# Attention scores: two heads from each half of the partitions, products that alternate between the halves, and a PSUM copy placed behind the second maximum

## Chip, cores and metric

The kernel runs on one core of a Trainium2 chip. The time is the device time of one execution in microseconds (us); lower is better. TensorE is written PE in the profile, its weight loads PEld, VectorE DVE, ScalarE ACT, GpSimd POOL and SyncE, which issues the DMAs here, SP.

## What is computed

The input is 8 x 256 tokens of 256 features in float32. The whole is six residual blocks in a row: mixture of experts, a selective scan, the mixture again, a gated feed-forward, causal attention, and the feed-forward again. Only the attention is touched. Cut to that, the reference is:

```python
slopes = get_slopes(16)                                   # 16 heads of 16 features
q = split_heads(x @ Wq + bq); k = split_heads(x @ Wk + bk); v = split_heads(x @ Wv + bv)
attn = einsum('bhqd,bhkd->bhqk', q, k) / sqrt(16)
attn = attn + (-slopes[:, None, None] * (Tx - 1 - arange(Tx))[None, None, :])
attn = where(causal, attn, finfo(float32).min)
p = softmax(attn, axis=-1)
out = einsum('bhqk,bhkd->bhqd', p, v) ... @ Wo + bo
```

## The kernel before

The attention works on four chunks of 512 tokens, which are two sequences of 256. A unit is four heads of one sequence: `unit(n)` gives the chunk c, the block kb of 128 features (eight heads), the sequence b and the half, and there are 32 units in all, N = 32. The q and k rows of a head are stacked over partitions, as hi, hi and lo parts against hi, lo and hi parts, with two more rows for the position bias: 50 partitions, `ROWS`. `attn_stack` has one head of each pair in partitions 0 to 49 and the other in 64 to 113. A unit takes the four heads of one of these halves.

Queries and keys of a sequence are cut at 128. For each head there are three blocks of 128 x 128: the early queries against the early keys (bank 0 of PSUM), and the late queries against both (banks 1 and 2). What is above the diagonal gets -1e30 by a matmul of the identity (`one`) with the mask.

TensorE (`tensor`, line 1938) runs in iteration n: `scores(n + 2)`, a job of slot 0, `turn(n)`, `weigh(n - 1)`, a job of slot 1. `scores` (line 1975) makes four early products and their mask and signals `s_SA`; it waits for the second exponentials (`s_exp`) of the unit before, makes four late products and two masks, and signals `s_S`. `turn` (line 2000) transposes the twelve blocks of probabilities into banks 3, 4 and 5, and waits before each bank until it has been copied out; the third, t = 2, waits for `s_pt2.at(n)`, the copy of unit n - 1. `weigh` (line 2017) multiplies the transposed probabilities with v. A job, by the table `JOBS`, is one of: a projection of q or k for the next chunk (six matmuls of 512 columns), of v, the output projection, or four transposes of a layer norm ("ln").

VectorE (`vector`, line 2201) runs in iteration n, in this order: the reciprocal of unit n + 1, `first(n + 2)`, the row maxima over bank 0; `keep(n - 1)`, the copy of bank 5 into `attn_pT`, which signals `s_pt2`; `second(n + 2)`, the maxima over banks 1 and 2; then parts of the layer norm, the low halves of the outputs, and its share of the jobs (for q or k this is `rows_lo`, which waits for ScalarE's `rows_hi`).

ScalarE (`scalar`, line 2116) runs in iteration n: four exponentials over bank 0 (line 2156), four over banks 1 and 2 (line 2162), each after the respective maxima, then jobs and the copies of banks 3 and 4 (`keep`, line 2166). GpSimd divides the probabilities by their sums (line 1882), two calls a unit. SyncE brings the stacks of the next chunk in.

Each engine runs its instructions in the order in which they are written. Score banks 0, 1 and 2 exist once, banks 3 to 5 once too.

Of the kernel before, what the change touches and what calls it, by code (L numbers as in the profile page):

```python
# [22 lines left out]
P = 128  # L23
# [5 lines left out]
KB = HID // P  # L29
# [1683 lines left out]
class Attention:  # L1713
# [18 lines left out]
    def __init__(self, k, tag, ins, before, tail, rows, fixed):  # L1732
        self.k, self.ins, self.before, self.tail = k, ins, before, tail
        self.rows, self.fixed = rows, fixed
        k.kind = tag
        self.s_load, self.s_wh, self.s_wl = Sem(k, "load"), Sem(k, "wh"), Sem(k, "wl")
        self.s_fix, self.s_kept, self.s_fill = Sem(k, "fix"), Sem(k, "kept"), Sem(k, "fill")
        self.s_one, self.s_bo = Sem(k, "one"), Sem(k, "bo")
        self.s_in, self.s_hi, self.s_lo = Sem(k, "in"), Sem(k, "hi"), Sem(k, "lo")
        self.s_row = [Sem(k, f"row{i}") for i in range(2)]  # L1740
        self.s_stack = [[Sem(k, f"stack{i}_{kb}") for kb in range(KB)] for i in range(2)]
        self.s_SA, self.s_S, self.s_nA, self.s_nB = Sem(k, "SA"), Sem(k, "S"), Sem(k, "nA"), Sem(k, "nB")
        self.s_eA, self.s_exp, self.s_rec = Sem(k, "eA"), Sem(k, "exp"), Sem(k, "rec")
        self.s_p, self.s_T = Sem(k, "p"), Sem(k, "T")
        self.s_pt01, self.s_pt2, self.s_pv = Sem(k, "pt01"), Sem(k, "pt2"), Sem(k, "pv")
        self.s_vp, self.s_v = Sem(k, "vp"), Sem(k, "v")
        self.s_oH, self.s_oL, self.s_out = Sem(k, "oH"), Sem(k, "oL"), Sem(k, "out")
        self.prior, last = {}, ("v1", 0)
        for c in range(NCH):
            for u in range(self.UNITS):  # L1750
                for slot in range(2):
                    job = self.job(c, u, slot)
                    if job:
                        self.prior[job], last = last, job
        self.prior["out1", NCH - 1] = last

        a = Arena(k, tag)
        new = a.new
        self.pt = new("pT", [P, 2, 3, CHUNK])
        self.p0, self.p1 = new("p0", [P, 3, 4, P]), new("p1", [P, 3, 4, SEQ])  # L1760
        self.v = new("v", [P, 4, self.PAIRS, 3 * HD])
        assert a.off <= k.arena + Glu.FFN_LOW
        a.off = k.arena + Glu.FFN_LOW
        self.st = [new(f"stack{i}", [P, KB, 4, CHUNK], F32R) for i in range(2)]
        W = KB * HID
        self.wH, self.wL = new("w_hi", [P, 4 * W], F32R), new("w_lo", [P, 4 * W], F32R)
        assert a.off <= Glu.early_at(k)
        a.off = Glu.ffn_raw_at(k)
        self.raw, self.mraw = new("w_raw", [P, 4 * W]), new("mask_raw", [P, P])
        assert a.off <= k.nc.sbuf_usable_end  # L1770
        own = Arena(k, tag)
        own.off = k.gate_at
        new = own.new
        self.mask, self.one = new("mask", [P, P], F32R), new("ident_r", [P, P], F32R)
        self.bo = new("bo", [P, HID])
        self.bq, self.bk, self.bv = new("bq", [P, KB]), new("bk", [P, KB]), new("bv", [P, KB])
        self.bqs = new("bq_scaled", [P, KB])
        self.nm = new("neg_max", [P, 3, 8])
        self.sum, self.rec = new("p_sum", [P, 3, 8]), new("recip", [P, 3, 8])
        assert own.off <= k.gate_at + 4 * TOK  # L1780
        acc = Arena(k, tag)
        acc.off = k.acc_at
        self.fix = [acc.new(n, [64, CHUNK], t) for n, t in (("fix", F32), ("fix_hi", F32R), ("fix_lo", F32R))]
        acc.off = k.acc_at
        self.oH, self.oL = acc.new("o_hi", [P, KB, CHUNK], F32R), acc.new("o_lo", [P, KB, CHUNK], F32R)
        self.stH, self.stL = acc.new("rows_hi", [P, 2, CHUNK], F32R), acc.new("rows_lo", [P, 2, CHUNK], F32R)
# [10 lines left out]
    @staticmethod  # L1797
    def unit(n):

        c, u = divmod(n, 8)  # L1800
        return c, u // 4, u // 2 % 2, u % 2

    def weight(self, which, kb):
        at = (which * KB + kb) * HID
# [133 lines left out]
    def tensor(self, e):  # L1938
# [34 lines left out]
                self.guest("pe", e, c, 2 * n + 1)  # L1973

        def scores(n):
            c, kb, b, half = self.unit(n)
            r = slice(64 * half, 64 * half + self.ROWS)
            if n % 4 == 0:
                for i in range(2):
                    e.wait_ge(self.s_stack[i][kb].sem, self.s_stack[i][kb].at(96 * (c + 1)))  # L1980
            if n:
                e.wait_ge(self.s_eA.sem, self.s_eA.at(n))
            q, kk = self.st
            for x in range(4):
                e.matmul(ps[:, 0, x * P:(x + 1) * P], q[r, kb, x, b * SEQ:b * SEQ + P],
                         kk[r, kb, x, b * SEQ:b * SEQ + P], start=(x == 0), stop=False)
            m = e.matmul(ps[:, 0, :].rearrange("p (x t) -> p x t", x=4), self.one[:],
                         self.mask[:].unsqueeze(1).broadcast_to([P, 4, P]), start=False, stop=True)
            m.then_inc(self.s_SA.sem, 1)
            if n:  # L1990
                e.wait_ge(self.s_exp.sem, self.s_exp.at(n))
            for x in range(4):
                e.matmul(ps[:, 1 + x // 2, x % 2 * SEQ:(x % 2 + 1) * SEQ], q[r, kb, x, b * SEQ + P:(b + 1) * SEQ],
                         kk[r, kb, x, b * SEQ:(b + 1) * SEQ], start=(x % 2 == 0), stop=False)
            for y in range(2):
                m = e.matmul(ps[:, 1 + y, :].rearrange("p (x t) -> p x t", x=2)[:, :, P:], self.one[:],
                             self.mask[:].unsqueeze(1).broadcast_to([P, 2, P]), start=False, stop=True)
            m.then_inc(self.s_S.sem, 1)
# [16 lines left out]
                m.then_inc(self.s_T.sem, 1)  # L2015

        def weigh(n):
            c, kb, b, half = self.unit(n)
            e.wait_ge(self.s_v.sem, self.s_v.at(2 * c + b + 1))
            if n > 1 and half == 0:  # L2020
                e.wait_ge(self.s_oL.sem, self.s_oL.at(n // 2))
            for t in range(2):
                for x in range(4):
                    if t == 0 and x % 2 == 0:
                        e.wait_ge(self.s_pt01.sem, self.s_pt01.at(2 * n + x // 2 + 1))
                    elif x == 0:
                        e.wait_ge(self.s_pt2.sem, self.s_pt2.at(n + 1))
                    v = self.v[:, 2 * b + t, 4 * kb + x, half * HD:(half + 2) * HD]
                    at = 32 * x
                    if t == 0:  # L2030
                        m = e.matmul(ps[at:at + 32, 6, 0:SEQ], v, self.pt[:, n % 2, x // 2, x % 2 * SEQ:(x % 2 + 1) * SEQ],
                                     start=(half == 0), stop=False)
                    else:
                        m = e.matmul(ps[at:at + 32, 6, P:SEQ], v, self.pt[:, n % 2, 2, x * P:(x + 1) * P],
                                     start=False, stop=(half == 1))
            m.then_inc(self.s_pv.sem, 1)

        e.wait_ge(self.s_fill.sem, self.s_fill.at(16 * 6 * KB))
# [162 lines left out]
    def vector(self, e):  # L2201
# [28 lines left out]
        def first(n):  # L2230
            e.wait_ge(self.s_SA.sem, self.s_SA.at(n + 1))
            e.tensor_reduce(self.nm[:, n % 3, 0:4], ps[:, 0, :].rearrange("p (x t) -> p x t", x=4), AX_X,
                            ALU.max, negate=True).then_inc(self.s_nA.sem, 1)
# [32 lines left out]
        for n in range(self.N):  # L2266
            c, u = divmod(n, self.UNITS)
            if n + 1 < self.N:
                recip(n + 1)
            if n + 2 < self.N:  # L2270
                first(n + 2)
            if 0 < n < self.N - 1:
                keep(n - 1)
            if n + 2 < self.N:
                second(n + 2)
            norm(c, u)
            job(c, u, 0)
            if n >= self.N - 2:
                keep(n)
            if n and n % 2 == 0:  # L2280
                out_lo(n // 2 - 1)
            job(c, u, 1)
            if n == self.N - 2:
                self.next.early_lo(e, 0)
# [248 lines left out]
def blocks(w, n=P):  # L2533

    return w.reshape(-1, n, w.shape[-1]).transpose(1, 0, 2)


def layout(inputs):
# [32 lines left out]
    out["state_pick"] = np.zeros((P, 2 * NST), f32)  # L2571
    out["state_pick"][:4 * NST] = np.tile(np.eye(2 * NST, dtype=f32), (2, 1))

    for name in "qkvo":
        out["W" + name] = blocks(a["L1_attn_W" + name]).reshape(P, -1)
    for name in "qkv":
        out["b" + name] = a["L1_attn_b" + name].reshape(-1, P).T
    out["bo"] = a["L1_attn_bo"]
    first = 2.0 ** (-2.0 ** -(np.log2(HEADS) - 3))
    slopes = np.array([first * first ** i for i in range(HEADS)], dtype=f32)  # L2580
# [30 lines left out]
```

## Time and profile before

| | |
|---|---|
| median of 3 timed runs | 1895.64 us (1895.43 to 1896.78) |
| profiled execution, span | 1896.9 us |
| PE busy | 1809.7 us, 95% |
| PEld busy | 1376.8 us, 73% |
| DVE busy | 1333.6 us, 70% |
| ACT busy | 947.0 us, 50% |
| POOL busy | 580.4 us, 31% |
| mean granted clock of TensorE | 0.992 |
| attention scores | 1558.8 to 1743.5 us of the span |

The shares are those of the whole span. The attention stage is a tenth of it and has limits of its own, so it is read by stretches and by the timeline. In a timeline a row is a run of like instructions: its start, how long it lasts, the engine, the line of the kernel, what is written from what, the shapes and the count; in brackets the idle time of the engine before it and what ended that. The starts of the first and last instruction of a row give the pitch when the duration of one is taken off; of products of the scores one lasts 0.27 to 0.28 us, though they follow one another faster, since matmuls are pipelined.

### The profile page before, as it was taken

What the parts mean: (1) busy time and instruction counts of PE and PEld (TensorE: products, weight loads), DVE (VectorE), ACT (ScalarE), POOL (GpSimd) and SP (SyncE); (2) the same over time, 40 slices, a digit from 0 to 9 for tenths busy, and PEclk for the clock granted to TensorE, in tenths of its full rate; (3) what the DMA queues carried; (4) which work ended last, traced back from release to release, by engine and by line L of the source; (5) the groups of instructions that cost most, each with busy time, mean ns of one, the idle gap of its engine ahead of it and who ended that gap; (6) DMA issues with size and microseconds to landing.
All of it is one profiled execution on the core that took longest, in us unless ns stands there. A gap on an engine that the chain in (4) does not pass through costs nothing.

```text
span 1896.9 us, 26320 instructions
## 1 busy us (share of the span) xinstructions
PE 1809.7 (95%) x9417; PEld 1376.8 (73%) x9417; DVE 1333.6 (70%) x1870; ACT 947.0 (50%) x1782; POOL 580.4 (31%) x399
## 2 busy tenths in 40 slices
PE   7999999999799999988689999999999999999999
PEld 6888888888354545434267888888888887777888
DVE  6666666567999999999976666565675556666533
ACT  4442323333688677675445433233333338888422
POOL 1000234000489878898730000000000025555000
PEclk9999999999899999999999999999999999999999
DMA  5331344210222222223203233132221306553100
GB/s 197 91 98 66 97 146 136 64 62 23 65 75 68 72 73 73 72 68 114 72 17 79 70 95 105 65 104 63 64 80 42 64 1 143 109 107 71 41 12 23
DMA packets 84202, 146.40 MB, mean 77 GB/s; under 512 B 13864, under 2 KB 23720, under 8 KB 83560
## 3 DMA queue, kind: packets, MB, share of 16 engines
q1 hardware_dynamic: 84072, 144.72, 26.8%
q8 instruction: 75, 1.23, 0.3%
q14 instruction: 55, 0.45, 0.1%
HBM read 130.38 MB, written 14.29 MB: 76 GB/s over the span
## 4 chain that ended last, share of the span: by engine, by line
PE 72%; DVE 14%; issue 6%; ACT 4%; POOL 3%; DMA 1%; SPq 0%; DVEq 0%; POOLq 0%; ACTq 0%
PE psum L161 19%; PE psum L162 19%; PE psum L163 18%; DVE scan_state L1640 6%; PE psum L1459 5%; POOL scan_state L1230 2%; PE psum L2014 2%; PE psum L1383 1%; DVE scan_state L1647 1%; PE psum L1354 1%; DVE moe_hidden_lo L866 1%; DVE X L822 1%; ACT attn_p L2162 1%; PE psum L278 1%; PE psum L1443 1%
## 5 line engine op out<-in xcount | busy, mean ns | idle before, releaser
L1230 POOL TENSOR_TENSOR scan_state<-scan_delta_u,scan_B_rows 128x1024 f32<-128x1024 f32 x127 | 299.4, 2367 | 96.5 <-PE psum L1459 82.7
L793 ACT ACTIVATE moe_hidden_hi<-moe_hidden 128x512 fp32r<-128x512 f32 x200 | 126.5, 633 | 400.0 <-DVE moe_hidden L846 399.1
L161 PE MATMUL psum<-xnT_hi,moe_w_hi 128*128 128x512 f32 x800 | 316.1, 395 | 2.6 <-DVE xnT_lo L475 2.3
L162 PE MATMUL psum<-xnT_lo,moe_w_hi 128*128 128x512 f32 x800 | 314.1, 393 | 0.0
L163 PE MATMUL psum<-xnT_hi,moe_w_lo 128*128 128x512 f32 x800 | 311.9, 390 | 0.0
L1640 DVE TENSOR_TENSOR_SCAN scan_state<-psum,scan_state 128x1024 f32<-128x1024 f32 x128 | 292.2, 2283 | 4.2 <-POOL scan_state L1230 2.9
L842 DVE TENSOR_TENSOR moe_gated_up<-moe_gate_rows,psum 128x512 f32<-128x512 f32 x184 | 126.5, 688 | 210.3 <-PE psum L163 122.0
L1459 PE MATMUL psum<-scan_state,ident 128*128 128x512 f32 x512 | 245.9, 603 | 3.8 <-DVE scan_gated L1655 2.5
L423 POOL TENSOR_SCALAR rstd<-mean_var 128x2 f32<-128x2 f32 x48 | 10.6, 222 | 748.4 <-DVE mean_var L457 748.2
L161 PE MATMUL psum<-moe_w_hi,moe_hidden_hi 128*128 128x256 f32 x800 | 230.2, 288 | 3.9 <-DVE moe_hidden_lo L866 2.8
L163 PE MATMUL psum<-moe_w_hi,moe_hidden_lo 128*128 128x256 f32 x800 | 226.2, 283 | 0.0
L162 PE MATMUL psum<-moe_w_lo,moe_hidden_hi 128*128 128x256 f32 x800 | 226.1, 283 | 0.0
L1573 ACT ACTIVATE psum<-scan_delta,scan_A 128x510 f32<-128x510 f32 x256 | 165.9, 681 | 116.1 <-DVE scan_state L1640 113.3
L866 DVE TENSOR_TENSOR moe_hidden_lo<-moe_hidden,moe_hidden_hi 128x512 fp32r<-128x512 f32 x200 | 138.4, 692 | 74.1 <-ACT moe_hidden_hi L793 72.7
L787 ACT ACTIVATE moe_hidden<-psum 128x512 f32<-128x512 f32 x200 | 119.8, 599 | 137.2 <-PE psum L163 136.9
L163 PEld LDWEIGHTS psum<-xnT_hi,moe_w_lo 128*128 128x128 f32 x800 | 150.6, 188 | 32.9
L161 PEld LDWEIGHTS psum<-xnT_hi,moe_w_hi 128*128 128x128 f32 x800 | 151.3, 189 | 29.9 <-issue 3.9
L162 PEld LDWEIGHTS psum<-xnT_lo,moe_w_hi 128*128 128x128 f32 x800 | 151.4, 189 | 24.3 <-issue 0.2
L161 PEld LDWEIGHTS psum<-moe_w_hi,moe_hidden_hi 128*128 128x128 f32 x800 | 152.4, 190 | 17.6 <-issue 6.7
L1647 DVE TENSOR_TENSOR scan_state<-scan_state,psum 128x1024 f32<-128x1024 f32 x128 | 156.2, 1221 | 7.1 <-PE psum L1443 3.1
L162 PEld LDWEIGHTS psum<-moe_w_lo,moe_hidden_hi 128*128 128x128 f32 x800 | 152.5, 191 | 7.9 <-issue 1.4
L1459 PEld LDWEIGHTS psum<-scan_state,ident 128*128 128x128 f32 x512 | 97.5, 191 | 83.3 <-issue 68.8
(226 smaller groups left out, 3482.1 us busy)
## 6 DMA issues: line engine op xcount, KB each, us to landing
scan_B_rows<-scan_B SPq DMA_DIRECT2D x127, 256.0 KB, 3.1
moe_gate_rows<-gate_table SPq DMA_DIRECT2D x176, 128.0 KB, 3.0
moe_w_raw<-moe_pack SPq DMA_DIRECT2D x50, 384.0 KB, 3.9
attn_stack<-attn_rows SPq DMA_DIRECT2D x96, 128.0 KB, 5.6
moe_gate_rows<-gate_table SPq DMA_DIRECT2D x32, 224.0 KB, 3.0
ffn_w_raw<-ffn_pack SPq DMA_DIRECT2D x16, 384.0 KB, 4.1
moe_gate_rows<-gate_table SPq DMA_DIRECT2D x32, 160.0 KB, 2.6
moe_gate_rows<-gate_table SPq DMA_DIRECT2D x24, 192.0 KB, 2.8
```

What stands on the lines that cost most here:

```text
L161: e.matmul(out, wH, xH, start=start, stop=False)
L162: e.matmul(out, wH, xL, start=False, stop=False)
L163: return e.matmul(out, wL, xH, start=False, stop=stop)
L787: e.activation(self.hb[:, b, :], self.k.psum[:, 2 * b, :], ACT.Silu).then_inc(self.s_silu.sem, 1)
L793: e.activation(self.hH[:, b, :], self.hb[:, b, :], ACT.Copy).then_inc(self.s_hH.sem, 1)
L842: e.tensor_tensor(self.tu[:, b, :], self.gp[:, at, :], k.psum[:, 2 * b + 1, :], ALU.mult).then_inc(self.s_tu.sem, 1)
L866: e.tensor_tensor(self.hL[:, b, :], self.hb[:, b, :], self.hH[:, b, :].bitcast(F32), ALU.subtract).then_inc(self.s_hL.sem, 1)
L1230: e.tensor_tensor(self.st[q % self.NBUF][:], self.dtu[:, 2 * h:2 * h + 2, :], self.Bs[:, q % self.RING, :].unsqueeze(1).broadcast_to([P, 2 ...
L1459: x = e.matmul(ps[:, 4 + m, :], k.ident[:], self.st[q % self.NBUF][:, m, :], start=(n == 0), stop=(n == NST - 1))
L1573: x = e.activation(ps[:, 2 * (q % 2) + m, :].rearrange("p (s t) -> p s t", s=2)[:, :, 1:], self.delta[:, i, :].rearrange("p (s t) -> p s t ...
L1640: e.tensor_tensor_scan(st, ps[:, b:b + 2, :].rearrange("p b t -> p (b t)"), st, 0.0, ALU.mult, ALU.add).then_inc(self.s_scan.sem, 1)
L1647: e.tensor_tensor(st[:], st[:], ps[:, 6, :].unsqueeze(1).broadcast_to([P, 2, CHUNK]), ALU.mult).then_inc(self.s_z.sem, 1)
```

## The change

- A unit now takes two heads of each half of the partitions instead of four heads of one half. `head(y, g)` gives, for y = 0 to 3, the partitions (y = 0, 1: the lower, y = 2, 3: the upper half) and the place in the stack. To fit, the columns of Wv and bv and the rows of Wo are put into another order when the inputs are laid out on the host.
- In `scores` the mask over bank 0 comes first and starts the accumulation there. Then comes the wait for `s_exp`, and then the eight products, early and late in one sequence, so that each is in the other half than the one before it, and in another bank than it. A new semaphore `s_left` makes the third early product wait for the second, since these two are in different halves and write the same bank. `s_SA` is signalled by the last early product, which is now the last of the eight. The two masks over banks 1 and 2 stay behind them.
- On VectorE `second(n + 2)` comes ahead of `keep(n - 1)`.

In `weigh` the name half becomes g, with no other effect there. The diff, cut:

```diff
@@ -1740,6 +1740,7 @@
+        self.s_left = Sem(k, "left")
@@ -1799,6 +1800,11 @@
+    def head(self, y, g):
+
+        half, x = y // 2, 2 * g + y % 2
+        return slice(64 * half, 64 * half + self.ROWS), x
@@ -1973,25 +1979,40 @@
         def scores(n):
-            c, kb, b, half = self.unit(n)
-            r = slice(64 * half, 64 * half + self.ROWS)
+            c, kb, b, g = self.unit(n)
...
             if n:
                 e.wait_ge(self.s_eA.sem, self.s_eA.at(n))
             q, kk = self.st
-            for x in range(4):
-                e.matmul(ps[:, 0, x * P:(x + 1) * P], q[r, kb, x, b * SEQ:b * SEQ + P],
-                         kk[r, kb, x, b * SEQ:b * SEQ + P], start=(x == 0), stop=False)
-            m = e.matmul(ps[:, 0, :].rearrange("p (x t) -> p x t", x=4), self.one[:],
-                         self.mask[:].unsqueeze(1).broadcast_to([P, 4, P]), start=False, stop=True)
-            m.then_inc(self.s_SA.sem, 1)
+
+            def early(y):
+                r, x = self.head(y, g)
+                return e.matmul(ps[:, 0, y * P:(y + 1) * P], q[r, kb, x, b * SEQ:b * SEQ + P],
+                                kk[r, kb, x, b * SEQ:b * SEQ + P], start=False, stop=(y == 3))
+
+            def late(y):
+                r, x = self.head(y, g)
+                return e.matmul(ps[:, 1 + y // 2, y % 2 * SEQ:(y % 2 + 1) * SEQ], q[r, kb, x, b * SEQ + P:(b + 1) * SEQ],
+                                kk[r, kb, x, b * SEQ:(b + 1) * SEQ], start=(y % 2 == 0), stop=False)
+
+            def masked():
+                e.matmul(ps[:, 0, :].rearrange("p (x t) -> p x t", x=4), self.one[:],
+                         self.mask[:].unsqueeze(1).broadcast_to([P, 4, P]), start=True, stop=False)
+
+            masked()
             if n:
                 e.wait_ge(self.s_exp.sem, self.s_exp.at(n))
-            for x in range(4):
-                e.matmul(ps[:, 1 + x // 2, x % 2 * SEQ:(x % 2 + 1) * SEQ], q[r, kb, x, b * SEQ + P:(b + 1) * SEQ],
-                         kk[r, kb, x, b * SEQ:(b + 1) * SEQ], start=(x % 2 == 0), stop=False)
+            early(0)
+            late(2)
+            early(1).then_inc(self.s_left.sem, 1)
+            late(3)
+            late(0)
+            e.wait_ge(self.s_left.sem, self.s_left.at(n + 1))
+            early(2)
+            late(1)
+            early(3).then_inc(self.s_SA.sem, 1)
...
@@ -2269,10 +2290,10 @@
                 recip(n + 1)
             if n + 2 < self.N:
                 first(n + 2)
+            if n + 2 < self.N:
+                second(n + 2)
             if 0 < n < self.N - 1:
                 keep(n - 1)
-            if n + 2 < self.N:
-                second(n + 2)
             norm(c, u)
...
@@ -2571,10 +2592,12 @@
+    order = np.arange(HID).reshape(KB, 2, 2, 2, HD).transpose(0, 3, 2, 1, 4).reshape(-1)
+    heads = {"Wv": a["L1_attn_Wv"][:, order], "Wo": a["L1_attn_Wo"][order], "bv": a["L1_attn_bv"][order]}
     for name in "qkvo":
-        out["W" + name] = blocks(a["L1_attn_W" + name]).reshape(P, -1)
+        out["W" + name] = blocks(heads.get("W" + name, a["L1_attn_W" + name])).reshape(P, -1)
     for name in "qkv":
-        out["b" + name] = a["L1_attn_b" + name].reshape(-1, P).T
+        out["b" + name] = heads.get("b" + name, a["L1_attn_b" + name]).reshape(-1, P).T
```

## Rows read from the trace of the kernel before

**Rows 1.** The head of the profile page.

```profile
span 1896.9 us, 26320 instructions
```

**Rows 2.** Busy by stretch: stretch, length; PE, PEld, DVE, ACT, POOL busy; clock, DMA.

```profile
1600.00:1650.00 50.00, 49.34 (x401) 37.75 (x399) 31.26 (x57) 42.46 (x158) 27.34 (x21) 1.00 0.55 106
```

**Rows 3.** Timeline, TensorE, unit at 1643.18: start us, us, engine, line, operation.

```profile
1643.18 0.66 PE L1985 MATMUL psum<-attn_stack,attn_stack 50*128 50x128 f32 x4
1643.77 0.50 PE L1987 MATMUL psum<-attn_mask,attn_ident_r 128*128 128x512 f32 x1
1644.20 0.74 PE L1993 MATMUL psum<-attn_stack,attn_stack 50*128 50x256 f32 x4
1644.87 0.50 PE L1996 MATMUL psum<-attn_mask,attn_ident_r 128*128 128x256 f32 x2
1645.21 1.47 PE L2014 MATMUL psum<-ident,attn_p 128*128 128x128 f32 x12
1646.61 0.64 PE L2031 MATMUL psum<-attn_pT,attn_v 128*32 128x256 f32 x8
```

**Rows 4.** Timeline, VectorE and ScalarE, the same unit.

```profile
1644.31 0.69 DVE L2232 TENSOR_REDUCE attn_neg_max<-psum 128x4 f32<-128x512 f32 x1 [0.22 <-PE psum L1987]
...
1644.92 0.68 DVE L2250 COPY attn_pT<-psum 128x512 f32<-128x512 f32 x1
...
1645.03 0.37 ACT L2156 ACTIVATE attn_p<-psum,attn_neg_max 128x128 f32<-128x128 f32 x1 [0.83 <-DVE attn_neg_max L2232]
...
1645.51 1.22 DVE L2237 TENSOR_REDUCE attn_neg_max<-psum 128x4 f32<-128x1024 f32 x1
...
1648.13 0.47 ACT L2162 ACTIVATE attn_p<-psum,attn_neg_max 128x256 f32<-128x256 f32 x1
```

**Rows 5.** Timeline, TensorE and VectorE, unit at 1648.97, behind a q job.

```profile
1648.97 0.66 PE L1985 MATMUL psum<-attn_stack,attn_stack 50*128 50x128 f32 x4
...
1649.80 0.76 DVE L2113 SCALAR_TENSOR_TENSOR attn_rows_lo<-psum,attn_bq_scaled,attn_rows_hi 128x512 fp32r<-128x512 f32 x1 [0.22 <-ACT attn_rows_hi L2106]
...
1650.58 0.64 DVE L2232 TENSOR_REDUCE attn_neg_max<-psum 128x4 f32<-128x512 f32 x1
...
1652.46 0.64 PE L2031 MATMUL psum<-attn_pT,attn_v 128*32 128x256 f32 x8
```

**Rows 6.** Timeline, VectorE, weight loads and TensorE, late in the stage.

```profile
1741.26 0.66 PE L1985 MATMUL psum<-attn_stack,attn_stack 50*128 50x128 f32 x4
...
1744.02 0.68 DVE L2250 COPY attn_pT<-psum 128x512 f32<-128x512 f32 x1
...
1744.75 0.42 PEld L2014 LDWEIGHTS psum<-ident,attn_p 128*128 128x128 f32 x4 [0.35 <-DVE attn_pT L2250]
...
1745.34 0.64 PE L2031 MATMUL psum<-attn_pT,attn_v 128*32 128x256 f32 x8
```

**Rows 7.** Timeline, TensorE, two products of a projection.

```profile
1648.20 0.39 PE L161 MATMUL psum<-xnT_hi,attn_w_hi 128*128 128x512 f32 x1
...
1648.43 0.39 PE L162 MATMUL psum<-xnT_lo,attn_w_hi 128*128 128x512 f32 x1
```

**Rows 8.** Timeline, TensorE, a unit with the transposes of a layer norm.

```profile
1654.83 0.66 PE L1985 MATMUL psum<-attn_stack,attn_stack 50*128 50x128 f32 x4
...
1658.70 0.64 PE L2031 MATMUL psum<-attn_pT,attn_v 128*32 128x256 f32 x8
```

**Rows 9.** Timeline, TensorE, the unit at 1592.52.

```profile
1592.52 0.66 PE L1985 MATMUL psum<-attn_stack,attn_stack 50*128 50x128 f32 x4
...
1594.24 0.74 PE L1993 MATMUL psum<-attn_stack,attn_stack 50*128 50x256 f32 x4 [0.64 <-ACT attn_p L2162]
...
1597.29 1.08 PE L2031 MATMUL psum<-attn_pT,attn_v 128*32 128x256 f32 x8
```

**Rows 10.** Timeline, TensorE, the last transposes.

```profile
1751.07 1.53 PE L2014 MATMUL psum<-ident,attn_p 128*128 128x128 f32 x12 [0.35 <-POOL attn_p L1882]
```

**Rows 11.** Busy time by stretch, the one with a fall of the clock.

```profile
1596.00:1600.00 4.00, 4.00 (x27) 2.64 (x26) 2.11 (x6) 2.97 (x13) 2.33 (x3) 0.58 1.09 148
```

More of the change, by code:

```diff
@@ L2017, in weigh @@
         def weigh(n):
-            c, kb, b, half = self.unit(n)
+            c, kb, b, g = self.unit(n)
             e.wait_ge(self.s_v.sem, self.s_v.at(2 * c + b + 1))
-            if n > 1 and half == 0:
+            if n > 1 and g == 0:
                 e.wait_ge(self.s_oL.sem, self.s_oL.at(n // 2))
@@ L2027, in weigh @@
                         e.wait_ge(self.s_pt2.sem, self.s_pt2.at(n + 1))
-                    v = self.v[:, 2 * b + t, 4 * kb + x, half * HD:(half + 2) * HD]
+                    v = self.v[:, 2 * b + t, 4 * kb + x, g * HD:(g + 2) * HD]
                     at = 32 * x
@@ L2031, in weigh @@
                         m = e.matmul(ps[at:at + 32, 6, 0:SEQ], v, self.pt[:, n % 2, x // 2, x % 2 * SEQ:(x % 2 + 1) * SEQ],
-                                     start=(half == 0), stop=False)
+                                     start=(g == 0), stop=False)
                     else:
                         m = e.matmul(ps[at:at + 32, 6, P:SEQ], v, self.pt[:, n % 2, 2, x * P:(x + 1) * P],
-                                     start=False, stop=(half == 1))
+                                     start=False, stop=(g == 1))
             m.then_inc(self.s_pv.sem, 1)
```

## Prediction

> **What bounds the kernel now.** Read the span first [rows 1]: 1896.9 us in the profiled execution, against a median of 1895.64 us of three timed runs (1895.43 to 1896.78). The profiled execution lies 1.3 us above the median; differences are worked out on the trace and put on the median. The change touches only the attention part, whose scores run from 1558.8 to 1743.5 us, so the second view is the busy time of that stretch [rows 2]: TensorE (PE) is busy 49.34 of 50 us. ScalarE has 42.46 us of work there and VectorE 31.26. So TensorE is what ends last in nearly every unit, and any new wait in its queue is lengthening, unless it takes the place of an older one.
>
> Third, one unit in the timeline. The loop of `tensor` runs scores(n+2), turn(n), weigh(n-1), a job. Take the unit whose scores start at 1643.18 [rows 3]; offsets below count from that start, o = 0. Four early products of 0.13 us pitch, the mask at 0.59, the late products at 1.02, two masks at 1.69, the twelve transposes of turn at 2.03, weigh at 3.43. VectorE in the same unit [rows 4]: first maximum at 1.13, copy of bank 5 (`keep`) at 1.74, second maximum at 2.33. The copy ends at 2.42. This matters because the last four transposes (t = 2) write bank 5 and wait for that copy (`s_pt2.at(n)`, line 2006). They are reached at about 2.03 + 8 x 0.11 = 2.91, so the copy is 0.5 us early and nobody sees the wait. In a unit that follows a q or k job [rows 5] VectorE is held by `attn_rows_lo` and starts the first maximum at 1.61; there the copy ends at about 2.84, just as the transposes need it. Near the end of the stage the wait is seen in the open [rows 6]: the copy starts at 1744.02, the weight load of the four transposes comes 0.73 us later after 0.35 us of idle time put down to that copy, and weigh starts 0.59 us after the load. From the start of the copy to weigh it is 1.32 us when the copy ends last.
>
> **The change, part by part.**
>
> *Heads in another order.* The same count of loads, matmuls, transposes and copies, with the same shapes; the weights of v and o are permuted ahead of the launch. DMAs and SP's queue don't change. Cost nothing, and no cover is needed.
>
> *The score block.* Before: products, mask, products, masks. From the mask's start to the next product it takes 0.43 us, though the mask streams 512 columns like a product of the projections, which follow one another in 0.23 us [rows 7]. The turn from a full-height operand to one of 50 rows so costs about 0.2 us. With the mask in front one such turn remains instead of two; the mask then follows full-height work. Unknown is the pitch of alternating products. Nearest rows: 0.11 us between transposes (1.47 us for twelve, less the last one's 0.27), 0.13 and 0.154 between products now (0.66 and 0.74 us for four, less the last one's 0.27 and 0.28) [rows 3]. I take 0.11: a transpose too brings a weight load of 128 columns for each 128 columns that it streams, and alternation makes these loads no fewer. If pairs ran fully side by side it would be half, about 0.06; if alternation did nothing, about 0.154. With 0.11: mask at 0, first product at 0.43, last product at 0.43 + 0.77 = 1.20, its end (`s_SA`) at 1.47, masks at 1.40, transposes at 1.74, all scores done at 1.90. TensorE alone saves 0.29 us a unit (0.07 to 0.64 by the other pitches).
>
> The row shows 0.2 us for a change of operand height. The Trainium skill, TensorEngine Tiling (Array Packing), Key Properties, says that changing the tiling mode drains the engine, and its Restrictions and Gotchas add that different row tiles must not use one bank at once, which is what `s_left` is for. In TensorE: Matmul & The Clock Gate, The mechanism, loads overlap running matmuls only where the row group differs. By that the pitch would be near the 0.06 end, and the sum below would be some 5 us smaller.
>
> *The wait on `s_left`.* TensorE waits for its own product early(1), three products back. It ends 0.27 us after its start and early(2) would come 0.33 us after it; cost 0, at most 0.2 us a unit if the load behind the wait can't be prepared. Behind it stand all later scores, and so the maxima.
>
> *The wait on `s_exp` moved ahead of all products.* Behind it now stand four early products more. The second exponentials end at 1648.6, 5.4 after the start of their unit and 0.35 before the next unit's scores [rows 4, 5]. Where the unit gets longer for the reason below, this wait vanishes.
>
> *The copy behind the second maximum.* This is the term that decides. VectorE now does first(n+2), second(n+2), keep(n-1), and second needs all of scores(n+2). Steps from [rows 4]: first to its successor 0.61 us (it lasts 0.69, and 0.64 where it comes late, which gives 0.55 [rows 5]), the second lasts 1.22 us, less the 0.09 by which successors overlap here (the copy lasts 0.68, its successor comes 0.59 later): 1.13 us. Two kinds of units:
> - after a q or k job, 12 of them: first still at 1.61 (VectorE is the late one, not the scores), second at 2.16, copy at 3.29, weigh at 3.29 + 1.32 = 4.61;
> - all others: first at 1.51 (0.04 after `s_SA`), second at 2.12, copy at 3.25, weigh at 4.57.
>
> TensorE is through with the eight other transposes at 1.74 + 0.88 = 2.62, so it waits about 1.3 us in each unit, with weigh(n-1), the job and scores(n+3) queued behind it.
>
> *Sum.* Start of weigh after start of scores, before, over n = 1 to 28: 13 units at 3.43 [rows 3], 6 at 3.49 [rows 5], 6 at 3.86 which hold four more transposes of a layer norm [rows 8], and three in which products or transposes wait already, the first at 4.77 [rows 9], the others at 4.20 and 3.80: 44.6 + 20.9 + 23.2 + 12.8 = 101.5 us. After: 12 x 4.61 + 16 x 4.57 = 128.4 us. Difference +26.9 us. What follows weigh in a unit is unchanged. At the front, two units that already wait for exponentials do all eight products after that wait: +0.5. At the end, the last transposes start at 1751.07 and hang on the chain from the last exponentials through the division on GpSimd [rows 10], 9.8 us after the start of the last scores; with no wait ahead of them these exponentials are done near 5.6, and the transposes can come at 8.9: -1.0. Together **+26.4 us**.
>
> *TensorE's clock.* It was granted 1.00 in the stage but for two falls to the lower of its levels (1.2 instead of 2.4 GHz), of which the second left 0.58 in 1596 to 1600 [rows 11]. It came shortly after TensorE had waited 0.64 us for the exponentials inside the score block at 1592.52 [rows 9], and the first, at 1572, after a like wait; the 0.35 us of [rows 6] brought none. In the unit at 1592.52 the fall shows as weigh at 4.77 instead of 3.43 + 0.64 of waiting, and as some 0.9 us more until the next scores: 0.9 to 1.6 us a fall, taken as 1.3. The changed kernel has 28 waits of 1.3 us. None falling costs nothing, all falling 28 x 1.3 = 36 us. I take 6 falls, 8 us: few, since the new wait stands beside transposes and near dense work, and part of a fall passes in the wait itself. Forecast: 1895.6 + 26.4 + 8 = **1930 us**, or 1.8% slower.
>
> **The rivals.**
>
> *A, the clock falls in most units.* For it: each unit has a longer hole than those that preceded a fall. Against: the wait of [rows 6] came with no fall, and the work around the new wait is the same transposes. 1895.6 + 26.4 + 36 = 1958 us.
>
> *B, alternation pays in full and the clock holds.* Pitch 0.06: first at 1.16 in the 16 units that VectorE doesn't hold, 0.35 us less each, -5.6: 1916 us. Even then weigh comes at 4.22, later than the 3.43 of now. The 0.07 end of the saving (alternation does nothing, so the change doesn't do what it says) puts first at 1.86, some 0.25 to 0.35 later in all 28: +8, 1930 without a single fall.
>
> *C, the other side: the copy isn't what TensorE waits for.* It decides from the point where something else holds the last transposes until 4.0 or later already; then only the saved 0.29 us of 30 units is left, -9: 1887 us. Against: the view shows that something else in no ordinary unit, and [rows 6] shows the copy itself as releaser. A part of it is to be expected in the six units of a layer norm, and is in the sum.
>
> *D, no change: ScalarE's loop takes over.* From the end of the second exponentials over products (1.2), first maximum (0.7) and both sets of exponentials (1645.03 to 1648.6 with 0.22 us of waiting in it, so 3.4) [rows 4] it is 5.3 to 5.6 us with the signals between them, against 5.8 of an ordinary unit now; if the copy cost nothing, this loop would leave some 0.15 us a unit, -4: 1892 us.
>
> **How the numbers follow.** A measurement tells about 0.2% (3.8 us) from no change. Chances: forecast (1920 to 1943) 0.60; B and sums near it (1908 to 1920) 0.18; A and sums above 1943 0.16; C 0.04; D, which lies within 0.2% or just beyond, 0.02. The range leaves out C, D and the upper part of A: 1908 to 1955. Faster 0.04, same 0.02, slower 0.94.
>
> **What would show it.** Right: among the waits a new large one, transposes (line of `turn`) released by the VectorE copy of `attn_pT`, 25 to 35 us in total over some 28 times; VectorE's copy starting 3.2 to 3.4 us after the mask; the mask of a unit 0.4 us ahead of its first product and products 0.11 us apart; waits of the products for the exponentials gone; the stage's granted clock a few per cent under one. Wrong: if TensorE is as dense as before in the stretch, the dependence was misread. If the waits are there and the time is off by over 10 us, the clock was mis-sized, and its column says so at once; if the spacing of copies is off, the pitch was.

## The result and the profile after

The changed kernel takes 1919.55 us (median of 4 runs, 1918.27 to 1920.32) against 1896.21 us for the kernel before beside it: a ratio of 1.0118, 95% interval 1.0105 to 1.0132; the medians lie 23.3 us apart. The profiled execution has a span of 1916.0 us:

```profile
span 1916.0 us, 26320 instructions
PE 1796.1 (94%) x9417; PEld 1364.5 (71%) x9417; DVE 1333.4 (70%) x1870; ACT 943.2 (49%) x1782; POOL 580.5 (30%) x399
```

The engines have the work of before, and TensorE is even 13.6 us less busy. The stage, read as in [rows 2], shows what happened (stretch, length, then PE, PEld, DVE, ACT and POOL busy, TensorE's clock, DMA):

```profile
1600.00:1700.00 100.00, 83.29 (x728) 62.43 (x728) 56.30 (x102) 74.99 (x282) 46.88 (x38) 1.00 0.49 92
```

Of 100 us TensorE is idle for 16.7, where it was idle for 1.3. The waits of the loop (engine and what it did, the releaser, us in total, times, the longest; a load and its matmul are listed apart for the same wait) name the cause. Before, waits of this kind came to 0.7 us of loads in all, in two units late in the stage, of which [rows 6] is one. After:

```profile
PEld psum L2035 <- DVE attn_pT L2271: 38.5, 27, 1.8
PE psum L2035 <- DVE attn_pT L2271: 32.1, 27, 1.5
```

Line 2035 is the transposes of `turn`, line 2271 the copy of bank 5 in `keep`. One unit of TensorE, to be read against [rows 3]; the products are now lines 1992 (early) and 1997 (late):

```profile
1629.56 0.39 PE L2001 MATMUL psum<-attn_mask,attn_ident_r 128*128 128x512 f32 x1
1629.88 0.32 PE L1992 MATMUL psum<-attn_stack,attn_stack 50*128 50x128 f32 x1
1629.89 0.38 PE L1997 MATMUL psum<-attn_stack,attn_stack 50*128 50x256 f32 x1
1630.05 0.27 PE L1992 MATMUL psum<-attn_stack,attn_stack 50*128 50x128 f32 x1
1630.11 0.38 PE L1997 MATMUL psum<-attn_stack,attn_stack 50*128 50x256 f32 x2
1630.38 0.32 PE L1992 MATMUL psum<-attn_stack,attn_stack 50*128 50x128 f32 x1
1630.38 0.38 PE L1997 MATMUL psum<-attn_stack,attn_stack 50*128 50x256 f32 x1
1630.54 0.27 PE L1992 MATMUL psum<-attn_stack,attn_stack 50*128 50x128 f32 x1
1630.74 0.51 PE L2017 MATMUL psum<-attn_mask,attn_ident_r 128*128 128x256 f32 x2
1631.09 1.03 PE L2035 MATMUL psum<-ident,attn_p 128*128 128x128 f32 x8
1633.33 0.66 PE L2035 MATMUL psum<-ident,attn_p 128*128 128x128 f32 x4 [1.20 <-DVE attn_pT L2271]
1633.91 0.64 PE L2052 MATMUL psum<-attn_pT,attn_v 128*32 128x256 f32 x8
```

and VectorE in it, against [rows 4]:

```profile
1630.85 0.69 DVE L2253 TENSOR_REDUCE attn_neg_max<-psum 128x4 f32<-128x512 f32 x1 [1.57 <-PE psum L1992]
1631.46 1.21 DVE L2258 TENSOR_REDUCE attn_neg_max<-psum 128x4 f32<-128x1024 f32 x1
1632.59 0.68 DVE L2271 COPY attn_pT<-psum 128x512 f32<-128x512 f32 x1
```

The transposes come 1.53 us after the start of the scores (2.03 before), stop after eight of twelve, and go on when the copy is out. Weigh starts at 4.35 instead of 3.43.

The account, from the first scores to the first product of the part that follows, in us:

| | before | after | difference |
|---|---|---|---|
| front, to the scores of iteration 2 | 23.19 | 26.14 | +2.95 |
| the 27 units from there, scores to weigh | 98.06 | 122.36 | +24.30 |
| the same units, weigh to the next scores | 61.16 | 56.11 | -5.05 |
| the end | 14.46 | 13.37 | -1.09 |
| the stage | 196.87 | 217.98 | +21.1 |

The work ahead of the stage was 2.05 us shorter in this execution, which the change doesn't touch, and what follows the stage is equal, so the spans differ by 19.1. The medians differ by 23.3. A span is some 2.4 us less than the time of the same execution; by that, an estimate, the profiled execution of before lies 3 us over its median, and that of after (1918.27 us) lies 1.3 us under its own, which is the difference.

### The profile page after: what moved, and what is told of

It reads as the page before. It is cut to its first block, busy times and chain, and to the rows that moved or that the text cites. A ratio compares the mean times of both kernels' runs of the same rounds, so it can differ in the third digit from the quotient of the medians.

```text
span 1916.0 us, 26320 instructions
## 1 busy us (share of the span) xinstructions
PE 1796.1 (94%) x9417; PEld 1364.5 (71%) x9417; DVE 1333.4 (70%) x1870; ACT 943.2 (49%) x1782; POOL 580.5 (30%) x399
## 4 chain that ended last, share of the span: by engine, by line
PE 70%; DVE 17%; issue 7%; ACT 3%; POOL 2%; DMA 1%; SPq 0%; DVEq 0%; POOLq 0%; ACTq 0%
PE psum L161 19%; PE psum L162 19%; PE psum L163 18%; DVE scan_state L1640 8%; PE psum L1459 4%; DVE attn_neg_max L2258 2%; POOL scan_state L1230 1%; PE psum L1383 1%; DVE scan_state L1647 1%; PE psum L2035 1%; PE psum L1354 1%; DVE moe_hidden_lo L866 1%; PE psum L2052 1%; DVE attn_pT L2271 1%; PE psum L278 1%
## 5 line engine op out<-in xcount | busy, mean ns | idle before, releaser
L162 PEld LDWEIGHTS psum<-xnT_lo,moe_w_hi 128*128 128x128 f32 x800 | 151.6, 189 | 24.3 <-issue 0.2
```

What stands on the lines that cost most here:

```text
L162: e.matmul(out, wH, xL, start=False, stop=False)
```

## The experiments

Each is compared with the kernel before on the same chip. The number of a unit is that of its iteration; "the stage" is the stretch of the account above.

**Is it the copy?** The order of VectorE was changed alone, in both directions, and the copy moved to a third place.

e2, on the kernel before (the conditions around these lines are left out in the short diffs):

```diff
             first(n + 2)
-            keep(n - 1)
             second(n + 2)
+            keep(n - 1)
```

> The kernel before with only VectorE's order changed: second maximum ahead of the copy of bank 5. Theory: all of the loss and more, since TensorE saves nothing in the score block: weigh at 4.6 to 4.7 after the start of the scores instead of 3.43 to 3.49, +1.13 to +1.25 us in 28 units, less 0.5 us in six units where a wait of the projection for the layer norm goes: 1923 to 1930 us. Rival (the loss needs the new score block): within 5 us of 1896.

Measured: 1922.39 us, ratio 1.0130 (1.0115 to 1.0145), 24 us slower, just under the range that was expected. A unit, in TensorE's timeline:

```profile
1620.56 0.66 PE L1985 MATMUL psum<-attn_stack,attn_stack 50*128 50x128 f32 x4
...
1622.59 1.03 PE L2014 MATMUL psum<-ident,attn_p 128*128 128x128 f32 x8
1624.66 0.66 PE L2014 MATMUL psum<-ident,attn_p 128*128 128x128 f32 x4 [1.04 <-DVE attn_pT L2250]
1625.25 0.64 PE L2031 MATMUL psum<-attn_pT,attn_v 128*32 128x256 f32 x8
```

Weigh is at 4.69 in every unit of the loop. Moving the copy by one place is enough for all of the loss; the new score block isn't needed for it.

e1, on the changed kernel:

```diff
             first(n + 2)
-            second(n + 2)
             keep(n - 1)
+            second(n + 2)
```

> The changed kernel with VectorE's order of before: first maximum, copy of bank 5, second maximum. Theory (the copy behind the second maximum is the whole loss): after the mask the first maximum starts at 1.3, the copy at 1.9 and ends at 2.6, the last four transposes are reached at 2.4, so the wait shrinks from about 1.3 to 0.2 us a unit; a unit takes 5.3 to 5.7 us and the kernel 1885 to 1892 us, faster than before. Rival (the alternating score block itself, with the mask in front and the late signal for the first maximum, is what costs): still over 1905 us.

Measured: 1900.2 us, ratio 1.0007 (0.9998 to 1.0016). The loss is gone, which rules the rival out, but the gain that was expected is not there either. In this trace an ordinary unit takes 5.53 us against 5.84; that gain comes in about half of the units. Behind a q or k job weigh is at 3.6 to 3.8, since the copy is still the last thing that the transposes wait for (7.8 us of load waits in the loop), and the units of a layer norm stay at 6.65 us. And the products, all eight of which now stand behind the wait for the second exponentials, wait 8.8 us for them in seven units, against 2.6 us in five before. The clock is no part of it: TensorE spent 6.8 us of the stage at the lower level, as before.

e3, on the changed kernel; e4 does the same to the kernel before:

```diff
             first(n + 2)
             second(n + 2)
-            if 0 < n < self.N - 1:
-                keep(n - 1)
+            keep(n)
             norm(c, u)
             job(c, u, 0)
-            if n >= self.N - 2:
-                keep(n)
```

> The changed kernel with the copy of bank 5 made in the unit's own iteration: first maximum, second maximum, copy of the same unit's bank 5 as soon as its transposes are through, so neither the next transposes nor the next weigh wait for it. Theory: TensorE has no wait, weigh at about 2.9 after the mask, a unit of 5.2 to 5.4 us against 5.8 before: 1878 to 1886 us. If ScalarE's loop (products to first maximum to exponentials to products) takes over first: 5.5 to 5.7 us a unit, 1886 to 1892 us. Rival (the score block itself costs): over 1896 us.

> The kernel before with the copy of bank 5 in its own iteration behind the second maximum, the control for the run above. Theory: TensorE never waited for the copy in an ordinary unit, so only the few units with waits gain: 1893 to 1896 us. Rival (the copy's place alone, not the new score block, brings a gain): under 1890 us.

Measured: e3 1891.09 us, ratio 0.9966 (0.9953 to 0.9979), and in a second set of runs 1892.28 us, 0.9968 (0.9956 to 0.9980); e4 1896.85 us, 0.9995 (0.9985 to 1.0005). So the copy's place alone brings nothing where TensorE never waited for it, and with it out of the way the new score block does bring some 6 us. That is less than the 1878 to 1886 us of the theory. The time lies in the range of the second one, but not for its reason: ordinary units take 5.25 us as forecast, not 5.5 to 5.7. What is missing is in two kinds of units. Those of a layer norm take 6.64. In one of them:

```profile
1631.15 0.66 PE L278 MATMUL psum<-ident,x_stage 128*128 128x128 f32 x4
1631.64 1.47 PE L2035 MATMUL psum<-ident,attn_p 128*128 128x128 f32 x12
1633.05 0.64 PE L2052 MATMUL psum<-attn_pT,attn_v 128*32 128x256 f32 x8
...
1634.56 0.50 PE L161 MATMUL psum<-xnT_hi,attn_w_hi 128*128 128x512 f32 x1 [0.66 <-DVE xnT_lo L475]
```

Twelve transposes without a hole, weigh at 3.63, but then the projection waits for the low half of the layer norm that it multiplies. The gain of these units is waited away there. It isn't only that the projection is reached earlier: in e4, with the score block of before, this wait is 0.59 us where it was 0.33, since the copy now stands ahead of the norm on VectorE. The second kind are seven units, three at the front, that of iteration 4 and three near the end, whose products wait for the second exponentials, 8.8 us in all as in e1.

**Where does the shorter score block come from?** e5 is e3 with `head` giving four heads of one half, and the weights in their first order:

```diff
-        half, x = y // 2, 2 * g + y % 2
+        half, x = g, y
```

> As e3_copy_own_unit, but the unit takes four heads of one half again, so the eight products keep their order and banks and no longer alternate between the halves of the partitions. Theory (the short score block comes from the alternation): pitch of the products 0.13 to 0.155 us instead of 0.094, their row 1.0 to 1.1 us long from first to last start instead of 0.66, weigh 0.25 to 0.45 us later, 4 to 10 us more than e3_copy_own_unit, 1895 to 1901 us. Rival (it comes from the mask in front and the single change of operand height): pitch and time as in e3_copy_own_unit, within 2 us.

Measured: 1896.4 us, ratio 0.9993 (0.9983 to 1.0002). Its products:

```profile
1622.89 0.39 PE L2001 MATMUL psum<-attn_mask,attn_ident_r 128*128 128x512 f32 x1
1623.21 0.32 PE L1992 MATMUL psum<-attn_stack,attn_stack 50*128 50x128 f32 x1
1623.38 0.33 PE L1997 MATMUL psum<-attn_stack,attn_stack 50*128 50x256 f32 x1
...
1624.17 0.22 PE L1992 MATMUL psum<-attn_stack,attn_stack 50*128 50x128 f32 x1
...
1624.66 1.47 PE L2035 MATMUL psum<-ident,attn_p 128*128 128x128 f32 x12
```

From the first to the last of the eight it is 0.96 us, against 0.66 in the unit of the changed kernel above, where twice two products of different halves show the same start (1629.88, 1630.38). From the start of the scores to the transposes: 2.03 before, 1.77 here, 1.53 after. So 0.26 us come from the mask in front, with one change of operand height in place of two, and 0.24 from the alternation. An ordinary unit takes 5.47 us against the 5.25 of e3, and the time is 5 us more, as the theory said; of the shorter score block each of the two theories explains a half.

**Does the price follow the hole, and what of the clock?** e6 and e10 put more VectorE work ahead of the copy in the changed kernel: the second maximum computed one more time, or half of it.

```diff
             e.wait_ge(self.s_S.sem, self.s_S.at(n + 1))
+            e.tensor_reduce(... ps[:, 1:3, :] (e10: ps[:, 1, :]) ...).then_inc(self.s_dose.sem, 1)
+            e.wait_ge(self.s_dose.sem, self.s_dose.at(n + 1))
             e.tensor_reduce(self.nm[:, n % 3, 4:8], ...
```

> The changed kernel with the second maximum computed twice, so that the copy of bank 5 comes another 1.2 us later and each hole of TensorE is 2.3 to 2.7 us long. Theory (the wait is the copy's place in VectorE's queue, and the clock isn't touched by holes among transposes): +1.15 to +1.3 us in each of 28 units, 1951 to 1957 us, granted clock of the loop 1.00. Rival (holes bring the clock down, only longer ones than 1.3 us): falls in most units, 0.9 to 1.6 us each on top, over 1970 us.

> The changed kernel with half of the second maximum computed once more, +0.65 us in VectorE's queue ahead of the copy, so the holes of TensorE are 1.9 to 2.1 us, between the 1.3 to 1.5 of the change and the 2.1 to 2.8 of e6_second_twice. If the clock falls in proportion to the added hole: about half of the falls of e6, +19 us for the holes and some +13 for the falls, 1947 to 1955 us. If there is a point below which no hole of this kind brings a fall and it lies above 2.1 us: +19 us alone, 1937 to 1941 us. If it lies under 1.9 us: falls as many as in e6, over 1960 us.

Measured: e6 1988.27 us, ratio 1.0475 (1.0460 to 1.0491); e10 1959.98 us, ratio 1.0339 (1.0321 to 1.0358). Over the changed kernel these are 69 and 40 us, for doses of 1.25 and 0.72 us a unit (weigh at 5.61 and 5.07 instead of 4.35), 34 and 19 us. The rest is the clock, told by the last but two of the columns; first e10, then e6:

```profile
1600.00:1700.00 100.00, 78.27 (x586) 58.61 (x586) 53.16 (x94) 62.95 (x235) 39.22 (x31) 0.86 0.48 90
```

```profile
1600.00:1700.00 100.00, 73.27 (x526) 53.23 (x526) 54.99 (x90) 57.78 (x216) 36.89 (x29) 0.85 0.42 80
```

Summed over stretches of 0.5 us, TensorE was at 1.2 instead of 2.4 GHz for 10 us of the changed kernel's stage, for 58 us of e10's and 99 us of e6's. The stage got 39.3 and 70.1 us longer; less the doses in 27 units 20 and 36 us are left, for 48 and 89 us more at the lower level: 0.41 us lost for each, in both. The holes of e10 are mostly 1.9 us, with some of 1.5 and 2.3. So for e6 the rival held, and the theory that holes among transposes leave the clock alone fell. The two stretches above look alike, but over the whole loop, the 27 units of the account, TensorE was at the lower level for 44 of 215 us in e10 (clock 0.90) and for 82 of 242 in e6 (0.83). By the falls it is the first case of e10, about half of those of e6; they cost 20 us where 13 had been put, so the time lies 5 us over that case's range and just under the third's. The second case, a point above 2.1 us under which no hole brings a fall, is out: of the ten falls that begin in the loop, six follow holes of 1.9 us. 0.7 us more of hole turned a loop without any fall into one with many. The longer hole also makes TensorE idle for a larger share of the unit; no run tells the length of a hole from that share.

e11 puts the dose of e10 into e3, where no transpose waits for a copy behind it.

> e3_copy_own_unit with the same extra half of a second maximum as e10_second_and_half, +0.65 us of VectorE work a unit, but no transposes waiting for a copy behind it. Theory (in e10 the added work acts through the copy that TensorE waits for, and brings the clock down through the longer holes): here the second exponentials come 0.5 us later and still end about when TensorE reaches the next products, no holes among the transposes, no more than the few falls of the clock at the front: 0 to 10 us more than e3_copy_own_unit, 1891 to 1901 us. Rival (VectorE work of that size costs wherever the copy stands): 19 us or more on top, over 1910 us.

Measured: 1901.16 us, ratio 1.0030 (1.0019 to 1.0042), some 10 us over e3 and just past the upper end of what was expected, where the same dose costs 40 us in e10. So it does act through the copy. The stage is 12.4 us longer than that of e3, and this comes out of three parts: the products wait 13.5 us in all for the second exponentials, in 21 units, where it was 8.8 in seven; the projections behind a layer norm wait 5.8 us where it was 4.0; and TensorE is at the lower level for 17.1 us, not 3.4, at 0.41 us each another 5.6, an estimate. The way from the second maximum over ScalarE to the next products had little slack left in e3.

**What else can be had.** e7 is e3 with the four early products ahead of the wait for the exponentials, e8 is e3 with both halves of the layer norm made earlier, e9 is e8 with the order of e7 in the seven units that had waited (in its list n is the argument of `scores`, which is the iteration plus 2).

e7:

```diff
             masked()
+            early(0)
+            early(1).then_inc(self.s_left.sem, 1)
+            e.wait_ge(self.s_left.sem, self.s_left.at(n + 1))
+            early(2)
+            early(3).then_inc(self.s_SA.sem, 1)
             if n:
                 e.wait_ge(self.s_exp.sem, self.s_exp.at(n))
+            late(0)
+            late(2)
+            late(1)
+            late(3)
```

> As e3_copy_own_unit, but the four early products stand ahead of the wait for the second exponentials and of the late ones (two lower, two upper, with the wait on s_left between them). Theory (the wait for the exponentials ahead of all products costs at the front of the stage and in the short units): the wait on s_left costs 0.15 to 0.3 us a unit, the front of the stage gives 1 to 3 us back, the three short units 0.3 each: 1886 to 1894 us. Rival (that wait costs nothing): 4 to 8 us slower than e3_copy_own_unit.

e8, first on ScalarE, then on VectorE:

```diff
+            job(c, u, 0)
             exps(n + 2, 0)
-            job(c, u, 0)
             exps(n + 2, 1)
...
             second(n + 2)
+            job(c, u, 0)
             keep(n)
             norm(c, u)
-            job(c, u, 0)
```

> As e3_copy_own_unit, but in the units of a layer norm ScalarE makes the norm's high half ahead of the first exponentials and VectorE its low half ahead of the copy. Theory: the projection behind it no longer waits 0.66 us for the low half in six units, 3 to 4 us less than e3_copy_own_unit, 1885 to 1889 us. Rival (ScalarE's loop bounds these units too): the wait moves to the next unit's products, within 1 us of e3_copy_own_unit.

e9, in `scores`, on e8:

```diff
+            if n in (1, 2, 3, 6, 28, 29, 31):
...
+            else:
```

> e8_norm_first, and in the seven units whose products waited for the second exponentials in e3_copy_own_unit (1, 2, 3, 6, 28, 29, 31) the four early products ahead of that wait as in e7_early_first. Theory (the gains lie in different units and add up, and less waiting at the front spares falls of the clock): 0.5 us less in each of four units of the loop, 1 to 3 us at the front: 1883 to 1889 us. Rival (what is gained in one place is waited for in the next, on ScalarE): within 1.5 us of e3_copy_own_unit.

Measured: e7 1890.1 us, ratio 0.9952 (0.9935 to 0.9969); e8 1889.17 us, 0.9960 (0.9946 to 0.9975). Neither is told from e3 by the time. In the trace of e7 an ordinary unit takes 5.54 us instead of 5.25, which pays for what the waiting units give back. In that of e8 the units of a layer norm take 5.9 to 6.1 us instead of 6.6 to 6.8 as meant, but the unit behind each takes 5.5 to 5.65 instead of 5.25: half of the gain moves on. e9: 1885.92 us, as expected, ratio 0.9938 (0.9926 to 0.9951), 10 us under the kernel before and 34 under the changed one. It is told from the e3 beside it (0.9968, 0.9956 to 0.9980); its interval overlaps those of e7 and e8. TensorE in its stage:

```profile
1600.00:1700.00 100.00, 99.03 (x888) 76.47 (x889) 69.31 (x123) 90.22 (x353) 58.17 (x45) 1.00 0.65 125
```

ScalarE is at 90% there. The stage has one fall of the clock, late; that of e3 has one in one execution and four in the other, with 189.1 and 192.3 us for the same program. A part of what e9 gains is that there was none at its front. Its stage takes 185.4 us with 3.4 at the lower level, that of the e3 beside it 192.3 with 13.7; at 0.41 us each the clock makes 4.2 of these 6.9 us. That is an estimate: the part was not tried apart.

## Why the prediction was right, and where it wasn't

The forecast was 1930 us, 34.4 slower, and 23.3 were measured: right in sign and mechanism, with the sum too high by 11 us. The time, 1919.55, lies half a microsecond under the forecast's own band (1920 to 1943, chance 0.60), in that of rival B and the sums near it (0.18). Term by term, in us; the prediction counts iteration 1 among its 28 units, the account counts it to the front, so its 1.1 us stand there:

| | forecast | measured |
|---|---|---|
| the 27 units, scores to weigh | +25.8 | +24.3 |
| the same, weigh to the next scores | 0 | -5.05 |
| front, with iteration 1 | +1.6 | +2.95 |
| end | -1.0 | -1.1 |
| clock | +8 | in the rows above |
| the stage | +34.4 | +21.1 |

The two terms that were off most, the clock and what follows weigh, were off the same way.

- **What bounds, and the copy as the term that decides: right.** The wait is where it was put, with the releaser that was named, in 27 of 27 units of the loop, and 32 us in all. e2 shows that this edit alone has the effect, e3 that the rest of the change is a gain without it.
- **The size of a unit: close, with two errors that cancel in part.** Ordinary units were put at 4.57 and came at 4.35; those behind a q or k job at 4.61 and came at 4.71. The pitch of alternating products was taken as 0.11 because each brings its load; it is 0.094 (0.66 us for seven steps), and the mask lets the first product follow after 0.32, not 0.43. So `s_SA` comes earlier and the first maximum starts at 1.29, not 1.51. Behind a q job VectorE is the late one, and since the scores start 0.1 us earlier behind the projection, its fixed place reads as 0.1 later. The copy of an ordinary unit so starts at 3.03, under the 3.2 to 3.4 that were to show it. The pitch lay between the 0.06 of rival B and the 0.11 that was taken. The Trainium skill (TensorE: Matmul & The Clock Gate, The mechanism) says that loads overlap running matmuls only where the row group differs. The trace agrees in direction: alternating, two pairs show one start each, though the other steps are 0.05 to 0.22 us, while products of one half are 0.14 us apart on average in e5.
- **"What follows weigh in a unit is unchanged": wrong, by 5 us.** Five projections stood idle 0.33 us each for the low half of a layer norm, which made weigh to the next scores 0.4 us longer than in a like unit without the wait; with the new wait ahead of them the operand is there (-2.0). The step from a job to the scores is 0.09 us shorter, 0.12 for 0.21 or 0.23 for 0.32, now that the mask, full-height like the job, comes first (-2.0). And the fall of the clock in the unit at 1592.52 [rows 9] didn't come again (-0.9). The first is the general case: a new wait covers an older one behind it.
- **The clock: the term that was mis-sized, +8 against about +1.** None of the holes in the loop, 0.9 to 1.5 us long, was followed by a fall. Both falls of the stage came at the front, each behind one of the two waits of 1.3 us for the exponentials, ahead of all the products:

```profile
1560.00:1564.00 4.00, 2.08 (x12) 1.23 (x10) 0.02 (x1) 3.99 (x18) 0.00 (x0) 1.00 0.00 0
1564.00:1568.00 4.00, 4.00 (x25) 3.84 (x23) 3.25 (x5) 2.50 (x12) 0.47 (x1) 0.63 0.57 219
```

  10 us at the lower level instead of 7, at 0.41 us each +1.4. The price of a fall was right (1.3 taken; the two of before held 6.8 us, which at 0.41 makes 1.4 each), their number was not: the trace of before has no holes among transposes of this length to read it from. e10 shows how near it was. With 0.7 us more of hole the clock cost 20 us, and with 1.25 us more, in e6, the 36 us of rival A.
- **The front: +2.95 for +1.6.** The wait for exponentials that now stands ahead of eight products shows as 1.3 us twice instead of 0.74 twice, and the longer time at the lower level comes on top. The front of e3, which differs in the copy's place alone, takes 24.3 us in two executions, with 3.4 and 6.8 us at the lower level; here it is 26.1, with 10. So 1.8 us of the 2.95 come with the copy's place or with the longer time at the lower level, and which of the two isn't told.
- **The end: -1.1 for -1.0, right.** The rivals C and D didn't come. That the measured value lies near B (1916) has half of B's reason, a clock that held; the pitch was 0.094 and not 0.06, and the rest is the shorter part behind weigh, which no rival had.
- **The level of before.** The prediction compares a span with a time and puts the profiled execution 1.3 us above the median; time with time it is some 3 us. No term hangs on it.

## What to carry to other kernels

A copy out of PSUM that looks free may be holding a buffer for the engine that bounds the kernel: before moving anything ahead of it on its queue, work out when the copy ends and when the bound engine next writes that bank, for the units where its queue is latest. A single buffer whose copy is made an iteration late has its slack in that queue; making the copy in its own iteration took it out of the path altogether, and only then did the saving in TensorE's own work reach the time. And take a saving on the bound engine as an upper limit: here 0.5 us a unit was saved and half of it was waited away for the layer norm and for ScalarE.

## What the runs showed of the hardware

- Products of 50 rows that alternate between partitions 0 to 49 and 64 to 113, with the banks different too, follow one another faster: eight in 0.66 us from first to last start, two pairs of them with one start, against 0.96 us in one half (e5).
- A mask of full height between products of 50 rows takes 0.43 us from its start to the next product; ahead of all of them, behind a projection of full height, 0.32 us.
- TensorE's clock in a loop of 7 to 9 us with one hole in each unit: holes of up to 1.0 us (e2) and of 0.9 to 1.5 us (the change) left it at 1.00 for 27 units, holes of mostly 1.9 us (e10) brought it to 0.90 on average over these units and of mostly 2.5 us (e6) to 0.83. A microsecond at the lower level cost 0.41 us in both.
- The copy's cost to TensorE is longer than the copy: from its start to the waiting transposes 0.73 to 0.74 us, and 0.58 to 0.59 more to the first product of weigh, the same before and after.
